# Two batches in each turn of both attention loops of a decoder layer

## The reference

```
x = x + self_attention(layernorm(x), w_qkv, w_out)                    # 16 heads of 32
x = x + cross_attention(layernorm(x), context, mask, Wq, Wkv, Wo)     # 16 heads of 64, 751 keys
x = x + ffn(layernorm(x), weight, gate, lora_U, lora_V)               # base + gated low-rank parts
```

## Time and profile before

| | us |
|---|---|
| median of 3 runs | 3515.34 |
| lowest and highest | 3514.51, 3515.39 |
| span of the profiled execution, first to last instruction | 3511.9 |
| PE busy in it | 3335.3 |

### The profile page before, as it was taken

The page is one execution under the profiler, slowest core; times in us unless marked ns, Lnnn a source line. Parts: engine busy times, 40 slices in busy tenths (PEclk is TensorE's granted clock), DMA queues, the critical chain, the costliest instruction groups (busy, mean ns, idle before and its releaser), DMA issues. The chain is left out here.

```text
span 3511.9 us, 72470 instructions
## 1 busy us (share of the span) xinstructions
PE 3335.3 (95%) x25084; PEld 2986.2 (85%) x25084; DVE 2222.4 (63%) x4888; ACT 1833.0 (52%) x4388; POOL 238.9 (7%) x324
## 2 busy tenths in 40 slices
PE   6999999998699999999999999999999999999798
PEld 6788888886488989889898898988989889899677
DVE  4666666664565756657575575755757566575487
ACT  4556555654345555555455455545555455454443
POOL 0000000000100000000000000000000000000154
PEclk8999999999799999999999999999999999999899
DMA  5554455445101001010100101101011010100133
GB/s 135 122 126 108 111 131 126 108 106 151 43 27 36 27 26 29 24 36 17 36 29 24 36 17 36 29 24 36 17 36 29 24 36 17 36 12 22 54 120 108
DMA packets 127475, 198.58 MB, mean 57 GB/s; under 512 B 18296, under 2 KB 69240, under 8 KB 126688
## 3 DMA queue, kind: packets, MB, share of 16 engines
q1 hardware_dynamic: 127200, 194.82, 21.1%
HBM read 99.35 MB, written 36.70 MB: 39 GB/s over the span
## 5 line engine op out<-in xcount | busy, mean ns | idle before, releaser
L1279 DVE CUSTOM_DVE_ANT_0 ca_prob<-ca_ps_s,ca_penalty 112x768 f32<-112x768 f32 x512 | 489.9, 957 | 532.8 <-PE ca_ps_s L1110 492.0
L1217 ACT ACTIVATE ca_probT<-ca_ps_t 128x448 f32<-128x448 f32 x512 | 277.7, 542 | 553.9 <-PE ca_ps_t L1121 550.3
L1210 ACT ACTIVATE ca_prob<-ca_prob,ca_low 112x768 f32<-112x768 f32 x512 | 476.6, 932 | 118.7 <-DVE ca_low L1279 114.7
L1095 PE MATMUL ca_ps_f<-ca_wkv_hi,ca_cnT_hi 128*128 128x256 f32 (+1 forms) x1536 | 444.4, 289 | 2.0 <-DVE ca_kstack L1322 2.0
L1095 PE MATMUL ca_ps_f<-ca_wkv_lo,ca_cnT_hi 128*128 128x256 f32 (+1 forms) x1536 | 431.9, 281 | 0.0
L1095 PE MATMUL ca_ps_f<-ca_wkv_hi,ca_cnT_lo 128*128 128x256 f32 (+1 forms) x1536 | 431.2, 281 | 0.0
L1121 PE MATMUL ca_ps_t<-ca_ident,ca_prob 112*128 112x112 f32 x3072 | 407.6, 262 | 1.5 <-ACT ca_prob L1210 0.5
L1121 PEld LDWEIGHTS ca_ps_t<-ca_ident,ca_prob 112*128 112x128 f32 x3072 | 337.4, 140 | 56.6 <-issue 29.9
L1244 ACT ACTIVATE ca_kstack<-ca_ps_f,ca_kbias 64x375 fp32r<-64x375 f32 x512 | 290.2, 567 | 180.0 <-PE ca_ps_f L1095 176.7
L1322 DVE SCALAR_TENSOR_TENSOR ca_kstack<-ca_ps_f,ca_kbias,ca_kstack 64x375 fp32r<-64x375 f32 x512 | 311.3, 608 | 99.2 <-ACT ca_kstack L1244 89.2
L1095 PE MATMUL ca_ps_f<-ca_cnT_lo,ca_wkv_hi 128*128 128x376 f32 x1024 | 342.5, 334 | 27.8 <-issue 27.8
(11 more groups left out here) (218 smaller groups left out, 7061.7 us busy)
## 6 DMA issues: line engine op xcount, KB each, us to landing
ca_q_raw<-q_T SPq DMA_DIRECT2D x128, 224.0 KB, 3.6
ca_cn<-in_ctx_dram SPq DMA_DIRECT2D x16, 1280.0 KB
sa_stack<-sa_qk_hi SPq DMA_DIRECT2D x64, 224.0 KB, 3.1
sa_stack<-sa_qk_lo SPq DMA_DIRECT2D x64, 224.0 KB, 3.5
sa_stack<-sa_qk_lo SPq DMA_DIRECT2D x128, 112.0 KB, 3.2
sa_stack<-sa_qk_hi SPq DMA_DIRECT2D x128, 112.0 KB, 3.0
q_T<-sa_q SPq DMA_DIRECT2D x16, 896.0 KB, 4.5
sa_xn<-in_x_dram SPq DMA_DIRECT2D x16, 448.0 KB, 3.6
```

Of the source, the lines that this page charges most:

```text
L1095: ins = nc.tensor.matmul(out, lhs[i], rhs[j], start=first_ and n == 0, stop=last_ and n == 2)
L1210: nc.scalar.activation(prob[:, h % 2, q, :], prob[:, h % 2, q, :], ACT.Exp, bias=low[:, h % 2, q:q + 1], scale=-1.0, accum_out=sums[:, h / ...
L1217: nc.scalar.activation(probT[:, h % 2, 2 * u:2 * u + 2, :], src[:, 0:2 * T].rearrange("p (k t) -> p k t", k=2), ACT.Copy).then_inc(TR.done ...
L1279: nc.vector.tensor_tensor_reduce(out=prob[:, h % 2, q, :].rearrange("p (c s) -> p c s", c=2), in0=ps_s[0:QT, :, 0:HALF], in1=penalty[:, :] ...
```

## The change

The loop of each engine does two turns in one. In self-attention 14 turns become 7 pairs; in cross-attention 15 turns become 7 pairs, and the fifteenth turn stands as straight code behind the loop. SP's loops get 6 and 7 pairs, and in self-attention one more turn as straight code. The tasks, their order and their waits are the same, with counts worked out from 2 * j + u.

```
-        with engine.Fori(0, TURNS) as t:
-            run(part["turn"], t + 1, ("turn", t))
+        with engine.Fori(0, TURNS // 2) as j:
+            for u in range(2):
+                run(part["turn"], 2 * j + u + 1, ("turn", 2 * j + u))
...
-                with sp.Fori(0, TURNS - 1) as t:
-                    next_input(t + 1)
-                    turn(t + 1, ("turn", t))
+                with sp.Fori(0, TURNS // 2 - 1) as j:
+                    for u in range(2):
+                        next_input(2 * j + u + 1)
+                        turn(2 * j + u + 1, ("turn", 2 * j + u))
+                next_input(TURNS - 1)
+                turn(TURNS - 1, ("turn", TURNS - 2))
                 turn(TURNS, ("turn", TURNS - 1))
...
+    PAIRS = TURNS // 2
...
-                with pe.Fori(0, TURNS) as b:
-                    run(table["tensor"], b, ("turn", b))
+                with pe.Fori(0, PAIRS) as j:
+                    for u in range(2):
+                        run(table["tensor"], 2 * j + u, ("turn", 2 * j + u))
+                run(table["tensor"], TURNS - 1, ("turn", TURNS - 1))
```

More of the change, by code:

```diff
@@ L229, in self_attention @@
     TURNS = B - 2
+    assert TURNS % 2 == 0
     def only(order, *kinds):
@@ L804, in cross_attention @@
     TURNS = B - 1
+    PAIRS = TURNS // 2
+    assert TURNS % 2 == 1
     table = {
@@ L1040, in _ @@
                 nc.gpsimd.memset(v_sb[96:P, :, KT - 1, :], 0.0).then_inc(fixed_ready, 1)
-                with pool.Fori(0, TURNS) as b:
-                    inverse_roots(pool, b + 1)
+                with pool.Fori(0, PAIRS) as j:
+                    for u in range(2):
+                        inverse_roots(pool, 2 * j + u + 1)
+                inverse_roots(pool, TURNS)
             @block.sync
@@ L1077, in turn @@
                     store(b, when)
-                with sp.Fori(0, TURNS - 1) as b:
-                    turn(b, ("turn", b), True)
+                with sp.Fori(0, PAIRS) as j:
+                    for u in range(2):
+                        turn(2 * j + u, ("turn", 2 * j + u), True)
                 turn(TURNS - 1, ("turn", TURNS - 1), False)
@@ L1261, in _ @@
                 run(first["scalar"], -1, ("first", 0))
-                with act.Fori(0, TURNS) as b:
-                    run(table["scalar"], b, ("turn", b))
+                with act.Fori(0, PAIRS) as j:
+                    for u in range(2):
+                        run(table["scalar"], 2 * j + u, ("turn", 2 * j + u))
+                run(table["scalar"], TURNS - 1, ("turn", TURNS - 1))
                 run(last["scalar"], TURNS, ("last", TURNS))
@@ L1360, in _ @@
                 run([t for t in first["vector"] if t[0] not in ("st", "ln")], -1, ("first", 0))
-                with dve.Fori(0, TURNS) as b:
-                    run(table["vector"], b, ("turn", b))
+                with dve.Fori(0, PAIRS) as j:
+                    for u in range(2):
+                        run(table["vector"], 2 * j + u, ("turn", 2 * j + u))
+                run(table["vector"], TURNS - 1, ("turn", TURNS - 1))
                 run(last["vector"], TURNS, ("last", TURNS))
```

## The result

The changed kernel takes 3509.93 us (median of 20 runs) where the kernel before, on the same chip, takes 3514.82 (20 runs): a ratio of 0.9986, with a 95% interval of 0.998 to 0.9992. That is 4.9 us less, within the 0.2% that the prediction calls no change, and 2.0 us under the predicted 3511.9. The sum came out right. Its terms did not: the two loops missed in opposite directions, by amounts that nearly cancel.

What follows compares the result with a forecast made beforehand. The prediction took PE, busy 3335.3 of 3511.9 us, as the bound. Its terms, -15.9 - 4.2 - 5.1 + 15.0 + 6.8 = -3.4 us, took the median from 3515.3 to 3511.9 us, range 3491 to 3525.

Steps and rivals of the forecast that it cites:

- Part 1: Cross-attention: 14 loop tops become 6, each removed one gives PE its 1.99 us, 15.9 us less.
- Part 2: Cross-attention's six remaining tops: PE's 2.0 us gap goes, a 1.3 us wait for ACT's copy comes; 4.2 us less.
- Part 3: Cross-attention: the three half-clock stretches on PE after gaps go, 1.7 us each, 5.1 us less.
- Part 4: Self-attention's six remaining tops: ACT alone refetches code, 3.0 us late, delaying PE's `T3` by 2.5 us each; 15.0 us more.
- third rival: Self-attention's tops: ACT's fetch queues behind other traffic, 4.5 us at `T3`, six clock drops; +12.0 us, 3527.3; chance 0.16.
- Part 5: Self-attention: half clock on PE after 4 of 6 tops at 1.7 us each, 6.8 us more.
- Part 6: Loops of SP and POOL stay short, under 128 instructions each, and cost nothing.
- page estimate: Code at loop branches: pages of 256 instructions, 128 for 8 KB packets; four small pages are kept, five are not.
- first rival: Self-attention keeps its code, so no stall or clock loss there: -25.2 us, 3490.1; chance 0.13.

Runs made afterwards that it cites:

- the shift: The kernel before, no loop paired, with 40 idle semaphore increments on PE ahead of the cross-attention's loop: 3486.56 us, and 3485.52 us when run again.
- The edit's halves: The kernel before with turns paired in cross-attention only: 3496.29 us; and with turns paired in self-attention only: 3506.29 us.
- the last kernel: The changed kernel with SP's stores behind the next input's load and 50 idle increments in ACT's code ahead of its self-attention loop: 3485.94 us.

## Why the prediction was right on the time, and where it was wrong

**Part 1, tops removed: right in size, and not a merit of the pairing.** All 27.8 us went, as parts 1 and 2 together said. But the 15.9 us put down to fewer tops would have come from the shift too. The edit's halves show it: alone they gain 19.5 and 9.5 us against the 3515.8 us of before in their comparison, and together 4.9. One takes away 8 of the 14 pauses and the other all 14; the same pause can be cured only once.

**Part 2, tops that stay in cross-attention: right mechanism, size off.** The page's edge moved away and ACT's copy became the wait. ACT's next instruction comes 2.5 to 2.7 us after its branch, where the step took DVE's 3.3. So PE stands 0.6 us and not 1.3: 3.4 us in six, against the 7.8 of the sum, which is 4.4 us more gain.

**Part 3, the clock in cross-attention: right.** The three stretches at 1.2 GHz are gone. 27.8 - 3.4 + 5.1 is 29.5 us of the 30.8, with 1.7 us a drop as the prediction took it; the remaining 1.3 is not traced.

**Part 4, tops in self-attention: the step that failed.** It said that "ACT alone pays" and took PE's branch as hidden, 4.05 us of queued work over 3.4 to 4.1 of fetch. The cover was right, and with the stores out of the way the branch takes 3.3 to 3.8 us and is hidden, as the last kernel shows. What was missed is the traffic at that moment. The step had an average share of the DMA engines over the whole stage and put it into the bound for ACT. The trace of before already had the two stores of 1,344 KB at that branch, and the engines at 1.02 in the 3 us behind it. The fetch of PE, which starts first, meets them; ACT's branch, 4.3 us later, doesn't. The pauses sum to 12.5 us, near the 15.0 of the step, but they stand ahead of `T2` and are PE's. That this size came out near was luck. This was near the prediction's third rival, with the roles turned: ACT's fetch among other traffic was named, PE's was not.

**Part 5, the clock in self-attention: the size failed.** Five of six tops have a half-clock stretch, against four taken. But four of the five last twice the 3.3 us of the cross-attention's row, so they are nine such lengths in all. By the row of before, where one length cost 1.7, that is up to 15.3 us against the 6.8 taken. With the 12.5 of pauses it makes 27.8, more than the 25.8 measured; some of it is idle time ahead of `T3` that shrank (7.0 us in place of 7.9), and 1.1 is not traced.

**Part 6, SP and POOL: right.** POOL's branch in self-attention still takes 45 ns, and inside the loops PE waits for POOL nowhere and for a DMA once, 0.2 us. Once, ahead of the cross-attention's loop, PE waits 25.9 us for POOL's `ca_v` where it was 23.1, but the stretch between the two loops is only 0.8 us longer.

**The sum.** Self-attention cost 25.8 and not 21.8, cross-attention gave 30.8 and not 25.2, and the stretch ahead gave 0.4. The misses of +4.0 and -5.6 hid each other, and that was luck. A time that comes out right is no proof of its terms; here only the place of the waits showed it.

**The page estimate held where it was tried.** "Four small pages are kept, five are not" was worked out from packet counts, and the shift of ACT's code by 50 instructions agrees with it. The first rival, that by size alone both bodies would be kept, did not come: ACT's 339 and PE's 1841 were both fetched again. The Trainium skill, "Runtime: NRT & Kernel Launch", section "Instruction fetch mechanics", calls the cost of crossing a 16 KiB boundary "mostly hidden". This trace agrees for the edges inside a body, and disagrees for one that lies 22 or 11 instructions behind a branch's target: 1.99 and 2.50 us at each turn. The section also says that a branch to a target outside the current two pages forces a fetch before execution goes on. The self-attention loop of before speaks against two pages: at the prediction's 256 instructions a page PE's 922 take four at least, and its branch costs 0.2 us.

## What to carry to other kernels

When an engine has an idle time marked "issue" a fixed number of instructions behind a loop's top, at every turn, look at where the top lies in the code before changing the loop. A few idle instructions ahead of it may do more than unrolling, though they cost time of their own where the engine is the late one (6.7 us for 40 here); and unrolling can push a body out of the memory that kept it. Where a long body's branch must be hidden, compare it with the queued work and also with what the DMA engines carry in the few microseconds behind the branch. When two engines are late at the same place, curing one shows little; try both before dropping either.

## What was not expected of the hardware

- A code fetch waits behind stores that are in flight. With 1,344 KB issued 1.4 to 2.3 us ahead of the branch, the first packet came 3.1 us after it and the branch took 5.5 us (5.9 in the median). With the DMA engines at a share of 0.02 it was 0.9 and 3.5 us.
- Thirty-nine instructions without work on PE, placed ahead of a loop, made a 3.5 ms kernel 0.9% faster, their own time included, and eleven made it 0.4% slower (one run).
- ACT keeps a loop of 339 instructions or fetches it at each turn, by where it begins: 0.3 or 2.5 us. PE's 922 stay and its 1841 don't; where its limit lies between them was not tried.
- After pauses of 1.9 to 2.5 us in self-attention PE's granted clock was 0.50 for 6.7 to 6.8 us in four cases of five, against 3.2 to 3.4 us in cross-attention. Why it is longer there stays open.
